# Flamingo cross-attention block on one core: the matmuls behind the row maxima of the scores, cut from a contraction of 128 rows to two of 64

## The chip, the cores and the metric

The kernel runs on one core of a Trainium2 chip. The metric is the device time of one execution in microseconds (us). Three executions without the profiler took 1800.39, 1806.55 and 1806.94 us, so the median is 1806.55 us. One more execution was recorded by the hardware profiler.

## What is computed

The input is `x` with 4 batches of 2048 rows of 512 features, and a context of 4 batches of 154 rows. Two residual steps follow each other:

```
x = x + tanh(g_xattn) * attention(layernorm(x), ctx)      # 16 heads of 32, 154 keys, softmax
x = x + tanh(g_ffn) * ffn(layernorm(x))                   # 512 -> 2048 -> 512, relu
```

The attention part is the one that the change touches:

```
q = layernorm(x) @ Wq.T + bq ;  k, v = split(ctx @ Wkv.T + bkv)
att = softmax(q_head @ k_head.T / sqrt(32))               # one 2048 x 154 matrix per batch and head
y = att @ v_head ; return y @ Wo.T + bo
```

In the feed-forward part the hidden values and the second weights are rounded to an 8-bit float format, and the output to a 16-bit one.

## The kernel before, in words

The 8192 rows of `x` are cut into 16 chunks of 512 rows (4 tiles of 128), 4 chunks to a batch. Most products are made of two float16 parts of each factor, high and low, in three passes (high times high, high times low, low times high), so one output bank of 128 x 512 costs 4 x 3 = 12 matmuls (`product`, L418; the profile's "ring" groups). The second feed-forward product has fp8 operands (`ffn_out`, L560).

**Order of the work.** Each engine has its own program, written out by hand from the same clock of "beats". A chunk starts 28 beats after the one before (`PERIOD = 28`), and tables such as `MAX_AT`, `LEFT_AT`, `MAIN_AT`, `VALUE_AT`, `O_AT`, `HIDDEN_AT` and `FFN_AT` say in which beats of a chunk each stage runs. Work of up to four chunks is interleaved that way. On TensorE one beat holds, in this order, `value`, `lift_left`, `lift_main`, `rank`, `query`, `project`, `hidden`, `ffn_out`, each if its table has the beat. Nothing reorders the work at run time; an engine that waits holds all that stands behind it.

**Row maxima.** Softmax needs a shift for each row and head. `rank(c, u)` (L466 to L480) makes it for 16 units of a chunk: `u` counts 4 groups `m` of 4 heads and 4 tiles `t` of 128 rows. The high part of the queries of the group, `qparts[:, 0, m, ...]`, has the 4 heads of 32 features in its 128 partitions. The moving operand is `kblk[:, m, :]`, where the keys of the 4 heads stand on a diagonal: head `h` in partitions 32h to 32h+31 and columns 154h to 154h+153, zero elsewhere. So one contraction over 128 partitions gives the scores of separate heads side by side. 4 x 154 = 616 columns don't fit one PSUM bank, so two matmuls of 308 columns each (heads 0 and 1, heads 2 and 3) write two banks, `m_ps[:, 0]` and `m_ps[:, 1]`, with the same stationary operand. The second one signals `scored`. On VectorE `row_max` (L800) reduces both banks to 4 maxima for each row and signals `maxed`; the next `rank` waits for it, as there is one pair of banks. Each call of `rank` is called a pair below; there are 16 x 16 = 256.

**Filling the diagonal.** GpSimd clears `kblk` at the start (L995), and `keys_diagonal` (L313 to L325) copies the diagonal blocks of a batch with 4 DMAs on SyncE's queue.

**Scores and values.** `shift_row` carries the negated maxima into row 96 of `qstack`. `lift_left` (L496) and `lift_main` (L503) compute the shifted scores from 97 rows. `lift_left` makes 4 matmuls, each with 32 columns of weights and its own 32 partitions of the output. `value` (L516, L519, L527, L530) sums the denominators and the values with groups of 4 such matmuls, 10 groups in a row. These are the kernel's only matmuls that take less than the whole width of the array. VectorE's `normalise` then takes the reciprocal of the denominators (L820) and scales (L823). `values_diagonal` (L343) and `keys_stacked` (L332) load a batch's other tables on SyncE's queue.

Of the kernel before, what the change touches and what calls it, by code (L numbers as in the profile page):

```python
# [7 lines left out]
F16 = mybir.dt.float16  # L8
# [7 lines left out]
P = 128  # L16
C = 512
KT = C // P
NH, DH = 16, 32
GH = P // DH  # L20
# [55 lines left out]
def build(nc, x, ctx_t, g_xattn, g_ffn, wq_t, bq, wk_t, bk, wv_t, bv, wo_t, bo, w1_t, b1, w2_t, b2, out):  # L76
    NB, NK = ctx_t.shape[2], ctx_t.shape[3]
# [5 lines left out]
    HK = 2 * NK  # L83
# [3 lines left out]
    with ExitStack() as es:  # L87
        def sb(name, shape, dt):
            return es.enter_context(nc.sbuf_tensor(name, shape, dt))
# [9 lines left out]

        kst = sb("kst", [P, 2, KT, NB * NK], F16)  # L100
        kcat = sb("kcat", [P, NH, KW], F16)
        kblk = sb("kblk", [P, KT, GH * NK], F16)
        vmain = sb("vmain", [P, NB, 2, C], F16)
        vleft = sb("vleft", [P, 2, C], F16)
        vblk = sb("vblk", [P, 2, KT, P], F16)
# [3 lines left out]
        qparts = sb("qparts", [P, 2, KT, CHUNK], F16)  # L109
# [61 lines left out]
        m_ps = es.enter_context(nc.psum_tensor("m_ps", [P, 2, 512], F32))  # L171
# [94 lines left out]
        def _(sp):  # L266
# [48 lines left out]
            def keys_diagonal(b, k):  # L315
                if b:
                    sp.wait_ge(scored, b * CPB * 16)
                else:
                    sp.wait_ge(kv_lo, KT)
                    sp.wait_ge(cleared, 1)  # L320
                if b == 2:
                    sp.wait_ge(kv_lo, EARLY + KT)
                for h in range(GH):
                    sp.dma_start(kblk[DH * h:DH * h + DH, :, h * NK:(h + 1) * NK],
                                 kst[DH * h:DH * h + DH, 0, :, b * NK:(b + 1) * NK]).then_inc(kblk_in, DMA)  # L325

            def keys_stacked(b, pair):
# [60 lines left out]
            for t in range(TILES):  # L388
                x_load(1, t)
            keys_diagonal(0, 0)  # L390
            q_stack(0, 0)
            keys_stacked(0, 0)
            for beat in range(FIRST, (NCH - 1) * PERIOD + LAST):
                run(shift_row, SHIFT_AT, beat)
                run(lambda c, t: x_load(c, t) if c > 1 else None, XLOAD_AT, beat)
                run(turn_x2, X2TURN_AT, beat)
                run(turn_x, XTURN_AT, beat)
                run(reload, RELOAD_AT, beat)
                run_batch(keys_diagonal, KBLK_AT, beat)
                run_batch(values_diagonal, VBLK_AT, beat)  # L400
                run(lambda c, pair: q_stack(c, pair) if c + pair else None, STACK_AT, beat)
                run_batch(keys_stacked, KST_AT, beat)
                if beat == STACK_AT[1]:
                    keys_stacked(0, 1)
                    values_diagonal(0, 0)
                run(store, STORE_AT, beat)
                once(w1_load, W1_LOAD, beat)
                once(w2_load, W2_LOAD, beat)
# [4 lines left out]
        def _(pe):  # L413
# [56 lines left out]
            def rank(c, u):  # L470
                m, t = divmod(u, TILES)
                pe.wait_ge(q_hi, c * KT + m + 1)
                if c + u:
                    pe.wait_ge(maxed, c * 16 + u)
                if u == 0:
                    pe.wait_ge(kblk_in, (c // CPB + 1) * GH * DMA)
                for half in range(2):
                    last = pe.matmul(m_ps[:, half, 0:HK], qparts[:, 0, m, t * P:t * P + P],  # L478
                                     kblk[:, m, half * HK:(half + 1) * HK], start=True, stop=True)
                last.then_inc(scored, 1)  # L480

            def lift_ready(c, m, u):
# [85 lines left out]
            for beat in range(FIRST, (NCH - 1) * PERIOD + LAST):  # L568
                run(value, VALUE_AT, beat)
                run(lift_left, LEFT_AT, beat)  # L570
                run(lift_main, MAIN_AT, beat)
                run(rank, MAX_AT, beat)
                once(keys_values, LATE_KV, beat)
                run(lambda c, m: query(c, m) if c else None, Q_AT, beat)
                run(project, O_AT, beat)
                run(hidden, HIDDEN_AT, beat)
                run(ffn_out, FFN_AT, beat)
# [500 lines left out]
```

## Time and profile before

| what | value |
|---|---|
| median of three executions | 1806.55 us (1800.39 to 1806.94) |
| the profiled execution, its own time | 1802.72 us |
| its span, first to last instruction | 1800.6 us |
| mean granted TensorE clock over the span | 0.950 of full speed |
| TensorE matmul busy | 1582.7 us (88%) |
| VectorE busy | 938.5 us (52%) |
| GpSimd busy | 874.6 us (49%) |
| ScalarE busy | 811.3 us (45%) |
| DMA engines, mean busy share by the queue's packets | 27.2% |

In the view of groups "busy" is the time in which at least one instruction of the group is under way, and "mean ns" is how long one takes from start to end; for matmuls that overlap, the second times the count is more than the first. In the timeline and in the chain of waits, the difference of two starts tells the pace. PEld rows are the loads of the stationary operand.

### The profile page before, as it was taken

The numbers are of one execution on the slowest core, as the hardware profiler recorded it, in microseconds if no ns is written. First come the engines' busy times: TensorE is split into PE (matmuls) and PEld (weight loads), VectorE is DVE, ScalarE is ACT, GpSimd is POOL, SyncE is SP. The second block draws the span as 40 slices with busy tenths as digits, with TensorE's granted clock in tenths as the row PEclk, the third lists the DMA queues.
The fourth block names the chain that finished last, engine by engine and source line by source line (L and its number), as shares of the span: only waits on it lengthen the run. The fifth ranks groups of instructions, "written<-read, shape, count | busy, mean of one in ns | idle before, by whom it ended". The sixth has DMA issues, their size and how long they took to land.

```text
span 1800.6 us, 24740 instructions
## 1 busy us (share of the span) xinstructions
PE 1582.7 (88%) x9372; PEld 711.3 (40%) x9372; DVE 938.5 (52%) x1181; ACT 811.3 (45%) x1180; POOL 874.6 (49%) x927
## 2 busy tenths in 40 slices
PE   2462458999997999999989999999989999999998
PEld 0220123444443444444433444444434444444443
DVE  5555463655555464646546564646445565636231
ACT  1233434545452545545443545455444535454511
POOL 2442463646445464646445564646445555645320
PEclk9776678999999999999999999999999999999999
DMA  6141232322324131323323231313232332312010
GB/s 209 56 112 57 78 77 53 72 75 68 81 67 90 41 90 48 80 74 77 86 59 77 57 97 39 91 48 80 83 66 71 77 77 58 79 37 66 29 48 24
DMA packets 220645, 128.36 MB, mean 71 GB/s; under 512 B 169328, under 2 KB 193904, under 8 KB 218864
## 3 DMA queue, kind: packets, MB, share of 16 engines
q1 hardware_dynamic: 220528, 126.78, 27.2%
q8 instruction: 75, 1.23, 0.3%
q14 instruction: 42, 0.34, 0.1%
HBM read 48.20 MB, written 16.78 MB: 36 GB/s over the span
## 4 chain that ended last, share of the span: by engine, by line
PE 70%; DVE 11%; issue 7%; SPq 6%; POOL 3%; DMA 2%; ACT 1%; DVEq 0%; POOLq 0%; ACTq 0%
PE ring L418 46%; PE ring L560 13%; DVE y L820 3%; PE m_ps L478 3%; PE s_ps L503 2%; DVE resid L860 2%; DVE bns L843 2%; PE y_ps L530 2%; PE y_ps L527 2%; SPq L332 2%; PE d_ps L516 1%; DVE smax L800 1%; SPq L302 1%; SPq L343 1%; PE d_ps L519 1%
## 5 line engine op out<-in xcount | busy, mean ns | idle before, releaser
L418 PE MATMUL ring<-late_a,w 128*128 128x512 f16 x3072 | 699.4, 380 | 9.2 <-DMA late_a<-x 9.2
L418 PEld LDWEIGHTS ring<-late_a,w 128*128 128x128 f16 x3072 | 297.9, 98 | 361.5 <-issue 25.9
L947 POOL TENSOR_TENSOR pmain<-p,pmain 128x512 f16<-128x512 f32 x256 | 302.9, 1185 | 169.1 <-ACT p L613 145.0
L634 ACT ACTIVATE late_b<-ring,b_sb,wsc 128x512 fp8e4<-128x512 f32 x256 | 199.3, 779 | 356.5 <-PE ring L418 356.5
L800 DVE TENSOR_REDUCE smax<-m_ps 128x4 f32<-128x616 f32 x256 | 202.8, 792 | 216.3 <-PE m_ps L478 216.0
L820 DVE RECIPROCAL y<-d_ps 128x512 f32<-128x512 f32 x64 | 214.6, 3353 | 105.2 <-PE d_ps L519 105.2
L613 ACT ACTIVATE p<-s_ps,prob_log,sc 128x512 f32<-128x512 f32 x320 | 247.4, 773 | 3.6 <-POOL pmain L947 3.6
L560 PE MATMUL ring<-w,late_b 128*128 128x512 fp8e4 x1024 | 234.9, 387 | 1.5 <-ACT late_b L634 0.9
L418 PE MATMUL ring<-xT,wq 128*128 128x512 f16 x768 | 186.4, 395 | 40.0 <-DVE wq L716 35.2
L947 POOL TENSOR_TENSOR pleft<-p,pleft 128x512 f16<-128x512 f32 x64 | 75.4, 1178 | 293.3 <-ACT p L613 286.1
L610 ACT ACTIVATE pmain<-s_ps,prob_log,sc 128x512 f16<-128x512 f32 x256 | 198.0, 773 | 6.4 <-PE s_ps L503 6.4
L478 PE MATMUL m_ps<-kblk,qparts 128*128 128x308 f16 x512 | 113.4, 304 | 76.7 <-DVE smax L800 74.8
L418 PE MATMUL ring<-wo,yT 128*128 128x512 f16 x768 | 177.3, 381 | 0.0
L647 ACT CAST x<-xn 128x512 f16<-128x512 f32 x64 | 39.6, 619 | 273.0 <-DVE xn L869 269.4
L560 PEld LDWEIGHTS ring<-w,late_b 128*128 128x128 fp8e4 x1024 | 101.5, 99 | 125.8 <-issue 10.3
L959 POOL TENSOR_TENSOR qparts<-q,qparts 128x512 f16<-128x512 f32 x64 | 79.3, 1239 | 118.3 <-ACT qparts L654 111.6
L839 DVE TENSOR_SCALAR q<-ring,sc,bias_s 128x512 f32<-128x512 f32 x64 | 51.8, 810 | 149.9 <-PE ring L418 137.1
L418 PEld LDWEIGHTS ring<-xT,wq 128*128 128x128 f16 x768 | 77.3, 101 | 130.6 <-DVE wq L716 35.2
L503 PE MATMUL s_ps<-qstack,kcat 97*128 97x512 f16 x256 | 99.4, 389 | 24.9 <-ACT p L613 24.9
L973 POOL TENSOR_TENSOR x<-xn,x 128x512 f16<-128x512 f32 x64 | 80.2, 1254 | 73.7 <-ACT x L647 73.7
L853 DVE TENSOR_SCALAR xin<-xin,mv,rs 128x512 f32<-128x512 f32 x64 | 49.9, 779 | 122.7 <-POOL rs L985 122.6
L418 PEld LDWEIGHTS ring<-wo,yT 128*128 128x128 f16 x768 | 75.5, 98 | 82.3 <-issue 2.2
(113 smaller groups left out, 1482.9 us busy)
## 6 DMA issues: line engine op xcount, KB each, us to landing
qstack<-qparts SPq DMA_DIRECT2D x384, 64.0 KB, 2.0
xin<-in_x SPq DMA_DIRECT2D x64, 256.0 KB, 3.1
resid<-in_x SPq DMA_DIRECT2D x64, 256.0 KB, 2.9
out_x<-resid SPq DMA_DIRECT2D x64, 256.0 KB, 2.3
resid<-in_w_t SPq DMA_DIRECT2D x4, 1024.0 KB, 4.9
xT<-x SPq DMA_TRANSPOSE x128, 2.5
late_a<-in_w_t SPq DMA_DIRECT2D x2, 1024.0 KB, 6.0
late_b<-in_w_t SPq DMA_DIRECT2D x2, 1024.0 KB, 7.0
```

The lines of the kernel that those rows point to most:

```text
L418: last = pe.matmul(dst, lhs(a, k), rhs(b, k), start=(k == 0 and p == 0), stop=(k == n_k - 1 and p == 2))
L478: last = pe.matmul(m_ps[:, half, 0:HK], qparts[:, 0, m, t * P:t * P + P], kblk[:, m, half * HK:(half + 1) * HK], start=True, stop=True)
L503: pe.matmul(s_ps[unit(c, m, 1 + h) % 2][:], kcat[0:97, GH * m + h, 0:P], qstack[0:97, GH * m + h, :], start=True, stop=True).then_inc(lift ...
L560: last = pe.matmul(ring_bank("f", c, t)[:], hT[:, j, t * P:t * P + P], w2[:, j, :], start=(j == 0), stop=(j == HT - 1))
L610: nc.scalar.activation(dst, s_ps[n % 2][:], ACT.Exp, bias=prob_log[:, 0:1], scale=sc[:, 7:8])
L613: nc.scalar.activation(p32[:, n % 2, :], s_ps[n % 2][:], ACT.Exp, bias=prob_log[:, 0:1], scale=sc[:, 7:8]).then_inc(exped, 1)
L634: nc.scalar.activation(hT[:, j, :], ring_bank("h", c, j)[:], ACT.Relu, bias=b1_sb[:, j:j + 1], scale=wsc[:, j // 4, 1:2], saturate=False). ...
L800: nc.vector.tensor_reduce(smax[:, heads, t].rearrange("p (a h) -> p a h", a=2), score_view, AX.X, ALU.max).then_inc(maxed, 1)
L820: nc.vector.reciprocal(y32[:], d_ps[:]).then_inc(inverted, 1)
L947: nc.gpsimd.tensor_tensor(part[:, 1, :], p32[:, n % 2, :], part[:, 0, :], ALU.subtract).then_inc(prob_lo, 1)
L959: nc.gpsimd.tensor_tensor(qparts[:, 1, m, :], q32[:], qparts[:, 0, m, :], ALU.subtract).then_inc(q_lo, 1)
L973: nc.gpsimd.tensor_tensor(x2_16[:, t % 2, 1, :], xn2[:], x2_16[:, t % 2, 0, :], ALU.subtract).then_inc(x2_split, 1)
```

## The change

`kblk` gets half as many columns: heads 0 and 1 stand in columns 0 to 307 of partitions 0 to 63, heads 2 and 3 in the same columns of partitions 64 to 127. `rank` keeps its two matmuls of 308 columns and their two banks, but the first contracts over partitions 0 to 63 alone and the second over 64 to 127, for both operands. The scores that come out are the same, since the rows left out of each contraction held zeros. The 4 DMAs of `keys_diagonal` carry the same bytes to other columns, and the clearing of `kblk` on GpSimd has half the elements. The order of the instructions is the same on all five engines; no wait and no signal is added, removed or moved. In the changed kernel lines from 478 on have a number higher by one.

```diff
-        kblk = sb("kblk", [P, KT, GH * NK], F16)
+        kblk = sb("kblk", [P, KT, HK], F16)
...
                 for h in range(GH):
-                    sp.dma_start(kblk[DH * h:DH * h + DH, :, h * NK:(h + 1) * NK],
+                    sp.dma_start(kblk[DH * h:DH * h + DH, :, h % 2 * NK:(h % 2 + 1) * NK],
                                  kst[DH * h:DH * h + DH, 0, :, b * NK:(b + 1) * NK]).then_inc(kblk_in, DMA)
...
                 for half in range(2):
-                    last = pe.matmul(m_ps[:, half, 0:HK], qparts[:, 0, m, t * P:t * P + P],
-                                     kblk[:, m, half * HK:(half + 1) * HK], start=True, stop=True)
+                    rows = slice(half * P // 2, (half + 1) * P // 2)
+                    last = pe.matmul(m_ps[:, half, 0:HK], qparts[rows, 0, m, t * P:t * P + P], kblk[rows, m, :],
+                                     start=True, stop=True)
                 last.then_inc(scored, 1)
```

## Rows read from the trace of the kernel before

**Rows 1.** The page: busy time by engine, and its slices (tenths).

```profile
PE 1582.7 (88%) x9372; PEld 711.3 (40%) x9372; DVE 938.5 (52%) x1181; ACT 811.3 (45%) x1180; POOL 874.6 (49%) x927
...
PE   2462458999997999999989999999989999999998
```

**Rows 2.** Waits of PE, 276 to 1700 us: engine, line, releaser; total us, times, longest.

```profile
PE m_ps L478 <- DVE smax L800: 34.7, 19, 3.5
PE d_ps L516 <- DMA vblk<-vleft: 17.1, 3, 6.0
PE d_ps L516 <- POOL pmain L947: 1.5, 1, 1.5
```

**Rows 3.** L478 alone by stretch: busy (instructions), PE clock, DMA share, GB/s.

```profile
60.00:276.00 216.00, 17.12 (x64) 0.69 0.30 82
276.00:1700.00 1424.00, 96.28 (x448) 0.99 0.27 69
```

**Rows 4.** Timeline of PE by start: two pairs between full-width products.

```profile
832.79 0.38 PE L503 MATMUL s_ps<-qstack,kcat 97*128 97x512 f16 x1
833.01 0.43 PE L478 MATMUL m_ps<-kblk,qparts 128*128 128x308 f16 x2
833.27 2.75 PE L418 MATMUL ring<-late_a,w 128*128 128x512 f16 x12
835.86 0.43 PE L478 MATMUL m_ps<-kblk,qparts 128*128 128x308 f16 x2
836.13 0.38 PE L418 MATMUL ring<-wo,yT 128*128 128x512 f16 x1
```

**Rows 5.** Timeline around the first and the last narrow group of a `value`.

```profile
818.00 0.81 PE L418 MATMUL ring<-late_a,w 128*128 128x512 f16 x3
818.74 0.40 PE L516 MATMUL d_ps<-pmain,ones 128*32 128x512 f16 x4
818.96 0.39 PE L519 MATMUL d_ps<-pleft,ones_left 128*32 128x512 f16 x4
...
820.69 0.39 PE L530 MATMUL y_ps<-pleft,vblk 128*32 128x512 f16 x4
820.90 0.39 PE L496 MATMUL s_ps<-qstack,kcat 97*32 97x512 f16 x4
821.23 2.76 PE L418 MATMUL ring<-late_a,w 128*128 128x512 f16 x12
```

**Rows 6.** Timeline of the weight loads at the same two places.

```profile
818.21 0.10 PEld L418 LDWEIGHTS ring<-late_a,w 128*128 128x128 f16 x1
818.74 0.10 PEld L516 LDWEIGHTS d_ps<-pmain,ones 128*32 128x32 f16 x4 [0.42 <-issue]
...
821.22 0.33 PEld L418 LDWEIGHTS ring<-late_a,w 128*128 128x128 f16 x3 [0.43 <-issue]
```

**Rows 7.** The chain of waits (start, us, what) at a batch's end.

```profile
518.39 0.33 PE d_ps L516 x4
518.72 0.22 PE d_ps L519 x4
...
520.66 0.22 PE s_ps L496 x4
520.88 2.70 PE ring L418 x12
523.58 0.22 PE s_ps L503
523.80 2.59 PE ring L418 x12
```

**Rows 8.** The chain of waits where it leaves PE and comes back, a chunk without a new batch.

```profile
642.18 2.60 PE ring L418 x12
...
644.80 0.76 DVE resid L860
...
651.35 3.36 DVE y L820
...
657.48 0.69 DVE smax L800
658.17 0.14 issue
658.31 0.42 PE m_ps L478 x2
```

**Rows 9.** Timeline of PE: the pairs of that chunk's stretch, and the wait.

```profile
604.18 0.44 PE L478 MATMUL m_ps<-kblk,qparts 128*128 128x308 f16 x2
...
644.60 0.43 PE L478 MATMUL m_ps<-kblk,qparts 128*128 128x308 f16 x2
...
650.04 0.44 PE L478 MATMUL m_ps<-kblk,qparts 128*128 128x308 f16 x2
...
653.12 0.43 PE L478 MATMUL m_ps<-kblk,qparts 128*128 128x308 f16 x2
...
658.31 0.42 PE L478 MATMUL m_ps<-kblk,qparts 128*128 128x308 f16 x2 [1.95 <-DVE smax L800]
```

**Rows 10.** The chain of waits at a batch's change.

```profile
526.39 0.23 PE s_ps L503
...
526.65 0.59 SPq L332
...
545.27 2.90 DMA resid<-in_x
...
561.26 0.70 DVE smax L800
```

**Rows 11.** The chain of waits, first 10 us.

```profile
0.72 1.12 POOL kblk L995
...
3.91 2.11 DVE kcat L877
```

**Rows 12.** The chain of waits where it passes through a pair at the lower clock.

```profile
199.71 0.67 PE m_ps L478 x2
```

## The prediction

> **What bounds the kernel now.** I read the page first. TensorE (PE) is busy 88% of the span, the other three compute engines about half, and from the eighth slice of 45 us on PE stands at 9 in nearly every slice, at 8 in the one before [rows 1]. So from about 276 us to 1700 us the pace of PE should set the time. The waits say whether it does: in these 1424 us PE waits 34.7 us for VectorE's maxima in 19 waits, 17.1 us for a DMA in 3 and 1.5 us for GpSimd, 53 us in all [rows 2]. Everything else is PE's own work, and a pair of `rank` that gets shorter or longer moves the end, unless one of those waits swallows it. 448 of the 512 matmuls of L478, 224 of 256 pairs, start in that stretch, at a granted clock of 0.99; the other 64 lie in the start of the kernel, at 0.69 [rows 3]. 224 pairs are 14 chunks of 16.
>
> What one pair costs is read from starts, not from durations. The view gives a pair 0.43 us, but the work behind it starts 0.26 to 0.27 us after the pair [rows 4]. So the pair holds the array 266 ns, 133 for each matmul. A 512-column matmul takes 216 ns by the same reading: 12 of them in 2.59 us [rows 4].
>
> **The change part by part.** It adds and removes no instruction. It changes four things.
>
> *The two halves.* They use separate rows of the array, so they could run side by side. The trace of before has nothing with separate rows, but it has the neighbour: groups of four matmuls on separate column strips of 32. Such a group follows the next after 0.22 us, as long as one full-width matmul of the same 512 columns [rows 5, 7]. All four run at once, and their starts are about 4 ns apart. If rows behave like columns, the pair holds the array 4 + 133 = 137 ns, and 129 ns are saved.
>
> *Going into and out of the narrow form.* The same groups have a price at either end. Three full matmuls start at 818.00 and the first narrow group at 818.74: 0.74 us where 3 x 0.216 = 0.65 are due, so 93 ns are lost going in [rows 5]. Going out, L496 starts at 820.90 and L418 at 821.23, 0.32 to 0.33 us where 0.22 is the pace; the chain shows the same as 2.70 us for a product of 12 that otherwise has 2.59 [rows 5, 7]. Taken from the last of the four, which starts 10 ns after the first, it is 313 ns, of which 213 are its columns: 100 ns from the last column to the next start, where full-width matmuls lose 2 or 3. The weight loads show why: in the steady stream a load runs ahead, beside the matmul before, but at both ends of a narrow stretch it waits 0.42 and 0.43 us and starts together with its own matmul [rows 6]. The array is emptied first. In `value` ten groups share two such edges. A pair of `rank` stands alone between full-width work and would pay both: 93 in, then 4 + 128 for the second half's start and columns, then 100 out, 325 ns against 266. **The price of an ordinary pair is then x = +59 ns.** The bounds are -129 ns (no edge costs anything, sides run together) and +188 ns (both edges, and the halves run one after the other, 129 more). I take +59, because the nearest rows show both the running together and the edges. The Trainium skill, TensorEngine Tiling (Array Packing), Key Properties, says that changing the tiling mode, and not just the tile, drains TensorE. By it the sum is the one below; the trace agrees for columns (the 93 and 100 ns) and has no row for 64-row tiles.
>
> *Which pairs count.* Of the 16 of a chunk, two have another price. One directly follows `lift_left`, a narrow group (as at 604.18) and one starts after a wait (658.31) [rows 9]. They don't pay the way in, or paid it already: 59 - 93 = -34 ns. Three count nothing: 644.60, 650.04 and 653.12 [rows 9]. There the chain leaves PE at 644.8 with the first product of `project`, runs over VectorE (residual, statistics, the reciprocal of 3.36 us, the maxima) and returns at 658.31 [rows 8]. PE waits 1.95 us at that point, and a PE that is late by 0.1 us waits 0.1 us less. That leaves 11 ordinary pairs. In the three chunks with a new batch the chain already leaves PE at 526.39, goes through SyncE's queue and a DMA and returns behind 561.26 [rows 10], and 4 more ordinary pairs are covered in each. Over the dense stretch: 14 x (11 x 59 - 2 x 34) - 3 x 4 x 59 ns = 8.13 - 0.71 = +7.4 us.
>
> *The start.* There the chain of waits mostly runs through other engines. It passes a pair once, 0.67 us at the lower clock [rows 12]; with its halves side by side and nothing ahead to be emptied it ends about 0.25 us sooner. -0.25 us. If nothing else is waited for there, ten such would be -2.5, if an edge costs more, 0; the term is small either way.
>
> *Clearing `kblk`.* 1.12 us on GpSimd, first in the chain, before VectorE's 2.11 us and the first statistics [rows 11]. Half the elements, half the time: -0.56 us if it reaches the end, 0 if the loads of the weights cover it. I take -0.56.
>
> *The diagonal's DMAs and the maxima.* Same bytes, same queue, same place in the queue; `row_max` reads the same two banks of 2 x 308 columns. Nothing. With sides together `scored` comes at 93 + 4 + 295 instead of 133 + 295 ns, 36 ns sooner, which is nothing for VectorE either.
>
> **Sum.** With x as the price in us: 14 x (11x + 2(x - 0.093)) - 12x - 0.81 = 170x - 3.4. For x = 0.059 that is +6.6 us. The profiled execution took 1802.72 us and would take 1809.3. It lies 3.8 us under the median of the three shown; the mean of all four known times is 1804.2, and from that the forecast is **1811 us**. From the median alone it would be 1813. A change within 0.5% (9 us) is about what a measurement of this kernel can't tell from none, so +6.6 is no measurable change, but close to the line: x above 73 ns crosses it.
>
> **Rivals.**
>
> *No edges.* The halves run side by side, and going from full rows to half rows costs nothing, because only the column strips need the array emptied. For it: the loads for full rows and for 97 rows already follow each other without loss (L503 before L478, 0.22 us) [rows 4]. Against it: 97 rows may simply count as the full array, and the edges of the column groups are plain. 13 pairs a chunk save 129 ns: -170 x 0.129 - 0.81 = -22.7 us, so 1781 us. The Trainium skill, TensorE: Matmul & The Clock Gate, Part 3, gives a span of one matmul plus about 4 ns for each further tile of a pack, which is this rival's pair and names no price for the edges. The trace agrees on the 4 ns, not on the edges.
>
> *The halves go one after the other, with both edges.* Then the narrow form gives nothing back: x = 188 ns, 170 x 0.188 - 3.4 = +28.5 us, so 1833 us. It would come about if the weight load of the second half could not run beside the first half's matmul, each load being 98 ns long (0.10 in [rows 6]). The same place, L478 between two full-width products, and a dearer edge (the way in now needs weights of 128 columns in two loads, where the narrow groups load 32) lead the same way. It decides from x = 73 ns on. Against it: the four loads of a column group start together with their matmuls and cost no more than the edge.
>
> *The change doesn't do what it says.* A contraction over 64 rows might be run as a full-width one with half its rows idle, in order, without edges. Then only the clearing remains: 1804 us. Against it: the second half starts at partition 64, and the array must be told so.
>
> **How the numbers follow.** Edges as with the column groups: 0.60. Its own range is 1803 to 1820, for x from 20 to 110 ns; a third of it lies above the line of 0.5%. No edges: 0.17. One after the other or dearer edges: 0.17. No effect: 0.06. Faster by over 0.5%: 0.17 + 0.02 = 0.19. Slower by over 0.5%: 0.22 from the forecast, 0.15 from the dear case, 0.37. Within: 0.36 + 0.02 + 0.06 = 0.44. The range has to reach to the case without edges, 1779, and takes in x up to about 160 ns, 1828; what is left out is most of the dearest case and what lies under 1779.
>
> **What would show it.** In the changed profile, between full-width products: (1) the start of a pair lies 0.31 us after the start of the 512-column matmul ahead of it, not 0.22; (2) the work behind starts 0.23 us after the pair, not 0.27; (3) the weight load of the pair and of what follows it starts with its own matmul, after an idle 0.3 to 0.4 us; (4) the duration of the two together drops from 0.43 to about 0.30 us; (5) the one wait a chunk for VectorE's maxima shrinks from 1.95 by some 0.1 us; (6) the pair behind `lift_left` ends sooner than before. If (2) shows 0.14 us and (1) 0.22, the case without edges holds; if the two together still take 0.43 us, the halves don't overlap. I am wrong in the size if an edge of the row form costs other than 93 to 100 ns, and in the sum if the waits of VectorE don't swallow the three pairs.

## The result and the profile after

Five executions of the changed kernel took 1814.46 to 1820.54 us, median 1817.83, against 1800.39 to 1806.94, median 1802.72, of the kernel before (the four known times and one more of 1802.60). The ratio is 1.0077, 95% interval 1.0056 to 1.0098. So the change makes the kernel slower by 0.8%, 14 to 15 us. The forecast was 1811 us and no measurable change, with a range of 1779 to 1828. The time lies in the range. The statement did not hold: 0.8% is over the line of 0.5% that the prediction drew, so the slowdown is a measurable one, and the sum of +6.6 us is less than half of what was measured.

The pair of matmuls does what the diff says. This is the timeline of TensorE (PE) in the changed kernel, two pairs between full-width products; the columns are start, length and the instruction. It answers to [rows 4].

```profile
740.77 2.54 PE L418 MATMUL ring<-late_a,w 128*128 128x512 f16 x11
743.24 0.30 PE L479 MATMUL m_ps<-kblk,qparts 64*128 64x308 f16 x2
743.47 2.76 PE L418 MATMUL ring<-wo,yT 128*128 128x512 f16 x12
746.17 0.30 PE L479 MATMUL m_ps<-kblk,qparts 64*128 64x308 f16 x2
746.41 0.39 PE L418 MATMUL ring<-wo,yT 128*128 128x512 f16 x1
```

Both halves together last 0.30 us, where the pair lasted 0.43 [rows 4], so they run side by side. The work behind starts 0.23 to 0.24 us after the pair instead of 0.266. But 12 matmuls from 743.47 to 746.17 take 2.70 us, and the same 12 took 2.59 in [rows 4]: time is lost on the way into the next pair, and a little at the start of the product. The weight loads of the same place answer to [rows 6]:

```profile
743.23 0.10 PEld L479 LDWEIGHTS m_ps<-kblk,qparts 64*128 64x128 f16 x2 [0.42 <-issue]
743.47 0.11 PEld L418 LDWEIGHTS ring<-wo,yT 128*128 128x128 f16 x2
```

No load runs ahead here any more: those of the pair come after 0.42 us of idle and start with the pair, and the next product's first load starts with its own matmul. From pair to pair, before: 2.85 us, of which 0.266 for the pair. After: 2.93.

The busy time of the pairs in the dense stretch went from 96.28 us [rows 3] to 68.57, by the same view of the changed kernel:

```profile
276.00:1700.00 1424.00, 68.57 (x448) 0.98 0.29 69
```

That is 28 us less work shown, and the time still rose by 15. The idle time at the edges doesn't belong to any instruction, so the busy time of a group tells nothing about it here. The wait for VectorE is still there, a little shorter than the 1.95 us of [rows 9]:

```profile
757.58 0.38 PE L504 MATMUL s_ps<-qstack,kcat 97*128 97x512 f16 x1
759.78 0.31 PE L479 MATMUL m_ps<-kblk,qparts 64*128 64x308 f16 x2 [1.82 <-DVE smax L801]
```

What the whole comes to is read from one pair to the same pair a chunk later, in a chunk without a new batch and without a stretch at the lower clock. The timelines of before (first two rows) and after:

```profile
690.94 0.43 PE L478 MATMUL m_ps<-kblk,qparts 128*128 128x308 f16 x2
...
787.15 0.43 PE L478 MATMUL m_ps<-kblk,qparts 128*128 128x308 f16 x2
```

```profile
693.78 0.30 PE L479 MATMUL m_ps<-kblk,qparts 64*128 64x308 f16 x2
...
790.80 0.30 PE L479 MATMUL m_ps<-kblk,qparts 64*128 64x308 f16 x2
```

96.21 us against 97.02: a chunk is 0.81 us longer (0.80 from the unrounded starts). 14 chunks make 11.2 us, less about 0.9 us that the waits at the three changes of batch cover, 10.3 us. The other 4 to 5 us are put down to time at the lower clock, below.

### The profile page after: what moved, and what is told of

It is laid out like the page before. It is cut to its first block, busy times and chain, and to the rows that moved or that the text cites. A ratio compares the mean times of both kernels' runs of the same rounds, so it can differ in the third digit from the quotient of the medians.

```text
span 1815.7 us, 24740 instructions
## 1 busy us (share of the span) xinstructions
PE 1595.5 (88%) x9372; PEld 674.5 (37%) x9372; DVE 939.3 (52%) x1181; ACT 812.3 (45%) x1180; POOL 871.9 (48%) x927
## 4 chain that ended last, share of the span: by engine, by line
PE 69%; DVE 11%; issue 7%; SPq 6%; POOL 4%; DMA 2%; ACT 1%; DVEq 0%; POOLq 0%; ACTq 0%
PE ring L418 45%; PE ring L561 13%; DVE y L821 3%; PE m_ps L479 2%; PE s_ps L504 2%; SPq L302 2%; DVE resid L861 2%; DVE bns L844 2%; SPq L332 2%; PE y_ps L531 2%; PE y_ps L528 2%; PE d_ps L517 1%; DVE smax L801 1%; SPq L343 1%; PE d_ps L520 1%
## 5 line engine op out<-in xcount | busy, mean ns | idle before, releaser
L418 PE MATMUL ring<-late_a,w 128*128 128x512 f16 x3072 | 700.4, 380 | 9.2 <-DMA late_a<-x 9.2
L418 PEld LDWEIGHTS ring<-late_a,w 128*128 128x128 f16 x3072 | 289.2, 98 | 369.1 <-issue 25.6
L561 PE MATMUL ring<-w,late_b 128*128 128x512 fp8e4 x1024 | 241.1, 394 | 1.5 <-ACT late_b L635 0.9
L418 PE MATMUL ring<-xT,wq 128*128 128x512 f16 x768 | 185.1, 393 | 40.1 <-DVE wq L717 35.5
L418 PE MATMUL ring<-wo,yT 128*128 128x512 f16 x768 | 177.6, 382 | 0.0
L479 PE MATMUL m_ps<-kblk,qparts 64*128 64x308 f16 x512 | 80.3, 308 | 77.0 <-DVE smax L801 74.9
L418 PEld LDWEIGHTS ring<-xT,wq 128*128 128x128 f16 x768 | 73.5, 101 | 133.4 <-DVE wq L717 35.5
L504 PE MATMUL s_ps<-qstack,kcat 97*128 97x512 f16 x256 | 99.2, 389 | 25.8 <-ACT p L614 25.8
L830 DVE TENSOR_TENSOR ffn<-ring,bq 128x512 f16<-128x512 f32 x64 | 44.1, 689 | 126.0 <-PE ring L561 124.8
```

Source lines behind the costliest of these rows:

```text
L418: last = pe.matmul(dst, lhs(a, k), rhs(b, k), start=(k == 0 and p == 0), stop=(k == n_k - 1 and p == 2))
L479: last = pe.matmul(m_ps[:, half, 0:HK], qparts[rows, 0, m, t * P:t * P + P], kblk[rows, m, :], start=True, stop=True)
L504: pe.matmul(s_ps[unit(c, m, 1 + h) % 2][:], kcat[0:97, GH * m + h, 0:P], qstack[0:97, GH * m + h, :], start=True, stop=True).then_inc(lift ...
L561: last = pe.matmul(ring_bank("f", c, t)[:], hT[:, j, t * P:t * P + P], w2[:, j, :], start=(j == 0), stop=(j == HT - 1))
```

## The experiments

The two theories at the start. **Edges:** everything comes from the halves being a form of their own, which the array enters and leaves empty; side by side they save 129 ns, the edges cost more. **Other parts:** some of the 15 us comes from the smaller table, from VectorE's timing or from the clock.

### The small table with full-width matmuls

```diff
-                    rows = slice(half * P // 2, (half + 1) * P // 2)
-                    last = pe.matmul(m_ps[:, half, 0:HK], qparts[rows, 0, m, t * P:t * P + P], kblk[rows, m, :],
+                    last = pe.matmul(m_ps[:, half, 0:HK], qparts[:, 0, m, t * P:t * P + P], kblk[:, m, :],
```

> The changed kernel with its small key table, but both matmuls of a pair contract over all 128 partitions again. It leaves out the separation of the heads: the columns hold the sum of two heads' scores, so the maxima are of sums. Theory (the whole cost lies in the edges around the row halves): as the kernel before, within 3 us of it, and about 1 us less if clearing the smaller table reaches the end; a pair stands 0.216 to 0.220 us behind the matmul ahead and the work behind it 0.266 us later. Rival (the smaller table, its DMAs or the shifted start of the kernel cost part of the 15 us): 3 to 6 us above before.

Measured: 1804.96 us against 1804.58 for before on the same chip, ratio 0.9998 (0.9989 to 1.0008). Within that interval, some 2 us, the table and its DMAs cost nothing. The shorter clearing gives nothing that can be seen either, and the trace of the changed kernel shows where its gain ends. In the first microseconds (start, length, instruction) it is there:

```profile
0.72 0.61 POOL L996 MEMSET kblk<- 128x616 f32 x1 [0.29 <-POOLq L1072]
...
5.54 0.69 DVE L844 BATCH_NORM_STATS2 bns<-xin 128x6 f32<-128x512 f32 x1
...
28.77 0.37 POOL L1007 PARTITION_ALL_REDUCE amax<-mag  x1 [5.63 <-issue]
```

In the kernel before the first statistics started at 6.06 us, so 0.52 us were won, but its all-reduce started at 28.43 us, sooner than here. In between stands the transposing DMA of the first tiles: 8.77 us in the chain of the changed kernel, 7.75 in that of before, and 8.87 in a second profile of before. It varies by more than what was won.

### Both halves on the same rows

```diff
-                    rows = slice(half * P // 2, (half + 1) * P // 2)
+                    rows = slice(0, P // 2)
```

> Both matmuls of a pair contract over partitions 0 to 63, into their two banks. It leaves out the scores of heads 2 and 3 of each group. Theory (two edges, and only separate rows run side by side): the second matmul starts about 131 ns after the first instead of 3.5, the price of an ordinary pair rises from +75 to about +203 ns, and with 182 priced pairs less 12 covered the time is 170 x 0.128 = 22 us above the changed kernel, about 1840 us. Rival (the matmuls of one strip can also overlap, or the edge comes from the step from strip to strip and not from the form): the time of the changed kernel, or under it.

Measured: 1833.53 us, ratio to before 1.0162 (1.0146 to 1.0177), 15.7 us above the changed kernel. The timeline of this kernel:

```profile
744.64 0.38 PE L504 MATMUL s_ps<-qstack,kcat 97*128 97x512 f16 x1
744.95 0.43 PE L479 MATMUL m_ps<-kblk,qparts 64*128 64x308 f16 x2
745.32 2.76 PE L418 MATMUL ring<-late_a,w 128*128 128x512 f16 x12
```

The way in is the same 0.31 us, so the edge belongs to the 64-row form and not to the step from strip to strip. The two matmuls last 0.43 us again, and the work behind starts 0.37 us after the pair instead of 0.24. The saving of the halves does come from their separate rows. A chunk without disturbance is 1.73 us longer than in the changed kernel, which would be over 22 us, as expected; the time rose less, since this kernel has 24 us at the lower clock after 285 us in its profile where the changed one has 44. Over all their executions the difference is 17 us (table below), and half of that is about the 6 to 8 us that are missing.

### The second eight units one beat earlier, in both kernels

```diff
-MAX_AT = [-10, -9, -8, -7, -6, -5, -4, -3, 2, 3, 4, 5, 6, 7, 8, 9]
+MAX_AT = [-10, -9, -8, -7, -6, -5, -4, -3, 1, 2, 3, 4, 5, 6, 7, 8]
```

With full-width pairs:

> The kernel before, with the second eight units of rank one beat earlier (beats 1 to 8 instead of 2 to 9), so that no rank stands behind the reciprocal of the first value. Nothing is left out. Theory (PE sets the pace and the wait of 1.95 us a chunk is its only regular one): the wait goes, 14 x 1.95 = 27 us less, about 1776 us, and with it the stretches at the lower clock after 276 us, up to some 10 us more. Rival (VectorE is late anyway and the next thing of PE waits for it): the wait moves to L503, L418 or L516 and the time stays within 5 us of before.

With the row halves:

> The changed kernel with the same move of the second eight units to beats 1 to 8. Nothing is left out. Theory (an ordinary pair costs 75 ns, and the wait for VectorE covers three of them): 13 or 14 ordinary pairs a chunk count instead of 11, so the distance to the moved kernel before is 14 x (14 x 0.075 - 2 x 0.017) less 1 at the start and less what batches cover = 12 to 13 us, with no share of the clock in it. Rival (part of the 15 us between the two kernels is that the row halves bring more stretches at the lower clock): the distance is 15 us or more, and the trace shows more such stretches than in the moved kernel before.

Measured: 1785.15 us with full width, ratio to before 0.9894 (0.9879 to 0.9909); 1797.93 us with halves, 0.9960 (0.9946 to 0.9975). The distance is 12.8 us, as worked out: chunks last 95.50 and 96.39 us, 0.89 more. Here no wait for the maxima covers a pair, and the lower clock appears only where a batch changes, so this is the price of the row halves with the least else in it. Some 0.1 us a chunk is still taken back: the waits of the second feed-forward product for VectorE come to 15.4 us with halves, against 17.0 below.

The first of the two beats both kernels of this study. It did not give the 27 us and more that were expected. The waits of PE in it, from 276 to 1700 us, answer to [rows 2]:

```profile
PE d_ps L516 <- DMA vblk<-vleft: 16.1, 3, 5.8
PE ring L560 <- DVE resid L860: 12.9, 28, 1.9
...
PE ring L560 <- DVE ffn L829: 4.1, 14, 0.3
PE m_ps L478 <- DVE smax L800: 1.9, 6, 0.5
```

The wait of L478 fell from 34.7 to 1.9 us. Half came back as 17 us of waits of the second feed-forward product for VectorE, which is late there anyway; net the waits are some 17 us shorter, without the one wait of 8.6 us for a DMA at 275 us, which the kernel before has too (9.2 us) and which falls just into this window. Both theories had half of it.

### One more pair next to a narrow group

In the moved schedule with halves, the ninth unit goes from beat 1 to beat 0, right behind `lift_left`.

```diff
-MAX_AT = [-10, -9, -8, -7, -6, -5, -4, -3, 1, 2, 3, 4, 5, 6, 7, 8]
+MAX_AT = [-10, -9, -8, -7, -6, -5, -4, -3, 0, 2, 3, 4, 5, 6, 7, 8]
```

> The changed kernel with its second eight units in beats 0 and 2 to 8, so that one more pair of each chunk directly follows the narrow group of lift_left. Nothing is left out. Theory (the edge into the narrow form is paid once for column and row strips alike): the pair in beat 0 costs about -17 ns instead of +75, so 14 x 0.092 = 1.3 us less than with beats 1 to 8, about 1796.5 us; in the trace its start lies 0.313 us behind L497, as any follower's does. Rival (columns to rows is an edge of its own beside the one that full-width work pays): the start lies 0.40 us or more behind L497.

Measured: 1795.39 us, against 1797.93 for beats 1 to 8 in another set of runs; their ranges are 1794.29 to 1796.14 and 1794.88 to 1798.61. The trace is plainer: from chunk to chunk it gains 0.10 us on the kernel with beats 1 to 8. Such a follower of a narrow group in its timeline:

```profile
746.79 0.39 PE L497 MATMUL s_ps<-qstack,kcat 97*32 97x512 f16 x4
747.11 0.30 PE L479 MATMUL m_ps<-kblk,qparts 64*128 64x308 f16 x2
747.35 2.76 PE L418 MATMUL ring<-wo,yT 128*128 128x512 f16 x12
```

0.32 us, no more than full-width work pays behind a column group (0.33 in [rows 5]). So each step measured here, from full width to columns, to 64 rows and back, and from columns to rows, costs one edge, and two edges don't add up in one place.

### The two kernels again

> The kernel before, unchanged, for a second profile. Theory A (which of the waits of 1.95 us is followed by a stretch at the lower clock is chance of the single execution): such stretches at other chunks than in the first profile, their total after 276 us anywhere between 25 and 48 us. Theory B (it hangs on the kernel): the same chunks, total 37 us within 3.

> The changed kernel, unchanged, for a second profile. Theory A (chance): other chunks, total after 276 us anywhere between 25 and 48 us, and the distance of the two medians is what the row halves cost, 170 x 0.075 - 3.4 = 9.4 us, up to about 2.5 more. Theory B (the halves bring stretches at the lower clock): again 44 us or more, against 37 for before, and a distance of 13 us or more.

Measured: 1803.72 us for before, 1818.84 us for the change, ratio to before 1.0072 (1.0053 to 1.0090). The record of the granted clock gives the time at 1.2 GHz between 285 and 1780 us: 37.5 us for the second profile of before (34.1 in the first), 44.4 us for the second of the change (44.4 in the first). Which waits of PE are followed by such a stretch differs between two profiles of one kernel, so Theory A is right on the place. On the amount B fits better: the change has 7 to 10 us more in each. Every execution also has its mean granted clock on record, and twice what is missing of the full clock, times the span, is its time at 1.2 GHz from first to last instruction. The 14 executions of the change have 184 us of it on average, 53 of before 175, most of it in the first 285 us. At half speed 9 us more cost 4.5 us, about what is missing between 10.3 and 14 to 15.

### A chunk made longer without edges

```diff
+                pe.matmul(m_ps[:, 0, 0:145], qparts[:, 0, m, t * P:t * P + P], kblk[:, m, 0:145],
+                          start=True, stop=True)
                 for half in range(2):
```

> The kernel before with full-width pairs and one more full-width matmul of 145 columns ahead of each pair, whose output the pair overwrites. It costs 145 / 2.4 + 2.5 = 63 ns a pair and no edge; 13 pairs a chunk count, so a chunk gets 0.82 us longer, as much as with the row halves (0.80). Theory T (how often a wait of some 2 us is followed by a stretch at the lower clock depends on how long a chunk is): the changed kernel's time and its total of such stretches, some 44 us between 285 and 1780 us, 13 to 15 us above before. Rival H (the row halves themselves, or the idle at their edges, bring the lower clock): the total stays at 34 to 37 us as in before, and the time is 14 x 0.82 less 0.8 = 10 to 11 us above before.

> The changed kernel, unchanged, on the same chip and in the same rounds as the padded one, for a comparison within 1 us and a third profile. Theory T: within 2 us of the padded kernel. Rival H: 3 to 5 us above it, and 44 us of stretches at the lower clock against 34 to 37.

Measured on one chip in the same rounds: 1812.93 us padded, ratio to before 1.0049 (1.0037 to 1.0062), and 1818.90 us for the change, 1.0089 (1.0074 to 1.0104). Chunks are as long as each other, 97.04 and 97.02 us. The padded kernel has 34.1 us at the lower clock, the change 47.8; over the whole span and all five executions of each it is 174 against 185 us. So the length of a chunk is not the cause at this length, and the two differ by 6 us with hardly anything but the clock between them. These are windows of 10 us behind the wait of four chunks; the columns are the window, its length, PE busy (instructions), granted clock, DMA share and GB/s. The change, first profile:

```profile
1060.00:1070.00 10.00, 8.18 (x32) 0.83 0.21 40
1160.00:1170.00 10.00, 8.62 (x33) 0.83 0.17 31
1460.00:1470.00 10.00, 8.18 (x32) 0.83 0.44 80
1560.00:1570.00 10.00, 8.18 (x32) 0.83 0.34 66
```

The padded kernel:

```profile
1060.00:1070.00 10.00, 8.23 (x42) 1.00 0.46 73
1160.00:1170.00 10.00, 8.23 (x41) 1.00 0.21 41
1460.00:1470.00 10.00, 8.23 (x42) 1.00 0.41 80
1560.00:1570.00 10.00, 8.23 (x41) 1.00 0.23 46
```

In three of the windows PE is busy for the same 8.2 us in both (8.6 in the other), with 1.8 us of wait. In the change the clock then fell to 1.2 GHz, for a third of the window (0.83), and 8 to 10 instructions fewer were under way in it (1 or 2 of them are the padding); in the padded kernel it stayed at 2.4 GHz. The windows are chosen: they are the plain chunks, those without a new batch, in which this profile has such a stretch. In the five profiles of the two kernels without padding such stretches follow 2 and 3 of the waits in plain chunks before, 4, 6 and 3 with the change; the padded kernel has none. What one costs shows in 16 matmuls of one kind behind a pair that waited 1.82 us. The change, first profile with such a stretch and third without:

```profile
1062.90 5.31 PE L561 MATMUL ring<-w,late_b 128*128 128x512 fp8e4 x16
...
1065.18 3.63 PE L561 MATMUL ring<-w,late_b 128*128 128x512 fp8e4 x16
```

1.7 us, half the length of the stretch, after the same wait.

### Do the halves always bring the lower clock?

The padded kernel with 463 columns instead of 145, and the changed kernel with the extra matmul of 145 columns ahead of its two halves.

> The kernel before with the extra full-width matmul ahead of each pair widened to 463 columns, 195 ns, so that a chunk is 2.5 us longer than before, 98.8 us, as long as with both matmuls on partitions 0 to 63 (98.76). Nothing has edges. Theory P (how many of the 2 us waits are followed by a stretch at the lower clock depends on the length of a chunk): the total between 285 and 1780 us is near the 24 us of that kernel. Theory H (it depends on what the pairs are): 34 to 37 us, as in all kernels with full-width pairs, and about 35 us above before less the covered pairs, 1836 to 1838 us.

> The changed kernel with one full-width matmul of 145 columns ahead of each pair, 63 ns, whose output the first half overwrites, so that a chunk is 0.82 us longer than in the changed kernel, 97.85 us. Theory H (the row halves bring the stretches at the lower clock): again 44 us or more of them, and 10 us above the changed kernel. Theory P (chunk length alone): another total, well under 44 us.

Measured: 1836.12 us (ratio 1.0175, 1.0158 to 1.0192) with 30.7 us at the lower clock, and 1824.98 us (1.0110, 1.0095 to 1.0125) with 20.5 us. In its profile the second speaks against "again 44 us or more": the same halves in a chunk of 98.14 us have less of it than the kernel before. But the execution in the profile is the one of four with the least: 160 us over the whole span, the others 171 to 182. The mean of 173 us is 11 us below the change, and whether it is below the 180 us of before in the same rounds is not shown, with a standard error of 5 us. Its time is 6 us above the changed kernel, where 10 were expected. A chunk grew by 1.1 us rather than 0.82, because the padding also parts the pairs behind `lift_left` and behind the wait from what stood ahead of them, and they now pay the way in (159 ns from the padding's start to the pair's, against 66 in the padded kernel with full width); the lower clock gave part of it back. The first, with full width and a chunk of 99.04 us, lies between the two theories on the clock.

The last column has the mean over the whole span and all executions (their number), worked out from the mean clocks; its standard error is 1 to 5 us.

| kernel | chunk, us | pairs | lower clock in the profile, after 285 us | whole span, mean |
|---|---|---|---|---|
| before, two profiles | 96.21 | full | 34.1, 37.5 | 175 (53) |
| small table, full width | 96.19 | full | 37.5 | 172 (10) |
| padded by 145 columns | 97.04 | full | 34.1 | 174 (5) |
| the change, three profiles | 97.02 | halves | 44.4, 44.4, 47.8 | 184 (14) |
| halves, padded | 98.14 | halves | 20.5 | 173 (4) |
| both on the same rows | 98.75 | 64 rows, in turn | 23.9 | 167 (4) |
| padded by 463 columns | 99.03 | full | 30.7 | 164 (4) |
| moved beats, full | 95.50 | full | 20.5 | 160 (4) |
| moved beats 1 to 8, halves | 96.39 | halves | 13.7 | 159 (5) |
| moved beats 0, 2 to 8, halves | 96.29 | halves | 23.9 | 158 (4) |

What is shown: the stretches begin in waits or shortly behind them, and with the wait of each chunk removed (last three lines) only those at the changes of batch are left. One profile tells little: the last two kernels differ by 10 us in it and not in the mean. For the change as made the stretches amount to 7 to 14 us more than before in three profiles of three, and to 9 us more in the mean of all executions. What stays open is the rule: neither the length of a chunk nor the form of the pairs gives the amount alone.

## Why the prediction was right or wrong

**What bounds the kernel.** Right. PE's pace sets the end, and what a pair costs goes through to the time: 63 ns of padding a pair made the kernel 8.5 us slower.

**The price of an ordinary pair: the term that was mis-sized.** The forecast had +59 ns from 93 in, 4 + 128 side by side and 100 out. The way in was right, 93 behind L504 and 96 behind L418. The way out, from the pair's start, was 236.5 ns (3.5 and 233) and not 232. And the first matmul of the product behind holds the second up by 226 to 227 ns instead of 215, 12 ns more; its weight load had not run ahead either, but that this is the reason is not shown. This was in the rows already: the chain has 2.70 us instead of 2.59 for the product behind a narrow group [rows 7], 0.11 us, which I read as the 100 ns. By the starts, an ordinary pair costs +75 ns. That is over the 73 ns at which the prediction put the line of 0.5%, and from which on, by its own words, the rival with dearer edges decides. So in size the dearer edges came true, by 2 ns; the reason that the rival gave for them, weights of 128 columns in two loads, was not tested.

**Which pairs count.** Right. Of the three pairs 644.60, 650.04 and 653.12 [rows 9] two are ordinary ones and the one at 650.04 follows `lift_left` too; together they make PE some 0.13 us later, and the wait takes it back, from 1.95 to 1.82 us. The timelines around a pair behind `lift_left`, before and after:

```profile
747.62 0.39 PE L496 MATMUL s_ps<-qstack,kcat 97*32 97x512 f16 x4
747.94 0.44 PE L478 MATMUL m_ps<-kblk,qparts 128*128 128x308 f16 x2
748.22 1.02 PE L418 MATMUL ring<-wo,yT 128*128 128x512 f16 x4
```

```profile
751.27 0.39 PE L497 MATMUL s_ps<-qstack,kcat 97*32 97x512 f16 x4
751.59 0.30 PE L479 MATMUL m_ps<-kblk,qparts 64*128 64x308 f16 x2
751.83 1.47 PE L418 MATMUL ring<-wo,yT 128*128 128x512 f16 x6
```

The way to the pair is the same 313 ns, and the work behind starts 237 ns after it instead of 277, so with the 12 ns above this pair costs -28 ns; the pair behind the wait costs -12. 11 x 75 - 28 - 12 = 0.785 us a chunk, measured 0.80. Without the wait the distance of the two kernels grew from 0.80 to 0.89 us a chunk.

**The start and the clearing.** -0.81 us were counted, and nothing that can be seen arrived; two profiles of the same kernel differ by some 2 us at the first wait of the dense stretch (357.6 and 359.6 us before). With x = 75 ns and this term at zero the prediction's own sum is 170 x 0.075 - 2.6 = +10.2 us, as the chunks show.

**What the sum left out.** The lower clock. The prediction named waits as things that swallow time and didn't ask what follows them. It is worth 4 to 5 us here: 10.2 + 4.5 = 14.7 us, of the 14 to 15 measured. The rows of before give a clock of 0.99 in the dense stretch [rows 3], so such time was there to be seen; how much more of it the change would bring could not be read from them.

**The rivals.** "No edges" is refuted: the way in is 0.31 us and not 0.22. "One after the other" too: 0.30 us for both, and the kernel that does run them in turn holds the array 0.37 us. The array did what the diff says. The Trainium skill says in TensorEngine Tiling (Array Packing), Key Properties, that a change of the tiling mode drains TensorE. The traces agree for 64-row tiles as well, at 93 to 96 ns in and about 105 ns from the last column out, and for a change from column tiles to row tiles, at the price of one edge.

**The marks.** (1), (2), (3), (4), (5) and (6) were all seen, (2) at 0.236 against 0.232 us. Median and range: 1817.83 in 1779 to 1828; it also lies in the 1803 to 1820 of the forecast case, near its top, though 4 to 5 us of it are clock, which no case had. So the range held with some luck. The chance of a measurable slowdown was 0.37 and should have been the largest: 59 ns stood 14 ns under the line, and each omission (the way out, the first product behind, the clearing, the clock) lay on the same side of it.

## What to carry to other kernels

Small contractions run side by side only save time if several of them stand together, since each step between full-width work and a part of the array cost some 0.1 us here, which no busy time shows. A lone pair of 308 columns saves 129 ns and pays 204. By these numbers two pairs in a row between full-width work would already save more than they pay, 258 against 204 ns; that is an estimate, and no run here has it. Price such a change from the starts of the neighbours, the first product behind included. Where an engine sets the pace and waits once a round for another, look at the order of the two before making the work smaller: one beat in a table gave 19 us, where half the rows of a matmul cost 14.

## What was not expected

- Between column tiles and row tiles there is one edge, 0.313 us from start to start behind `lift_left`, the same as to full width.
- The first matmul behind an edge holds up the second by some 10 ns more than elsewhere, whatever its form: 226 instead of 215 ns at full width and 512 columns; 141 ns for two 64-row matmuls of 308 columns on the same rows, and 140 to 142 for the full-width pair behind `lift_left`, where a full-width pair elsewhere has 130 to 134. Behind a wait it is 130 in either form.
- The changed kernel spent 44 to 48 us at 1.2 GHz after 285 us against 34 to 38 before, and a padded kernel with chunks of the same length 34; in one profile of the halves with more padding it was only 20. I have no rule for it.
